# A four-layer graph network on one core: the weighted sum with turned probabilities stationary, and projections in two fp16 passes

## What is computed

```python
h = relu(layernorm(x)); x = x + L0(h)      # and so on for L1, L2, L3
# L0, one head: softmax over the neighbours of q.k / 8, times v
Q, K, V = h @ W_q, h @ W_k, h @ W_v
out = softmax(where(adj == 0, -1e9, Q @ K.T / 8)) @ V
# L1, four heads, with biases
q = h @ Wq[head] + bq[head]                # k and v the same way
scores = leaky_relu(q @ k.T / 8, 0.2) + mask
out = leaky_relu(mean_over_heads(softmax(scores) @ v), 0.2)
# L2, additive: e[i,j] = sum_f a[f] * leaky_relu(u[i,f] + w[j,f]);  out = elu(softmax(e) @ hp)
# L3: e[i,j] = leaky_relu(src[i] + dst[j]); out = norm(elu(softmax(e) @ Wh + h @ W_res)) * gamma + beta
```

## Time and profile before

| | us |
|---|---|
| median of 3 runs | 3885.69 (3883.1 to 3893.41) |
| profiled execution | 3882.72 |
| its span, first to last instruction | 3880.8 |
| PE, DVE, ACT, POOL busy | 3269.0, 3276.1, 3046.8, 992.1 |
| four-head layer's loop | 1026 |
| additive layer's loop | 2066 |
| last layer's loop | 367 |

### The profile page before, as it was taken

How to read it: one execution, slowest core, us unless ns; L and a number is a source line. 1 busy time by engine, 2 the same in 40 slices (tenths; PEclk the granted TensorE clock), 3 DMA queues, 4 the chain that set the end, 5 groups by cost and what they waited for, 6 DMA issues and landing times. The chain is left out here.

```text
span 3880.8 us, 81004 instructions
## 1 busy us (share of the span) xinstructions
PE 3269.0 (84%) x31339; PEld 1730.1 (45%) x31339; DVE 3276.1 (84%) x6456; ACT 3046.8 (79%) x3649; POOL 992.1 (26%) x565
## 2 busy tenths in 40 slices
PE   7997999999999968888788887887887878878776
PEld 5664666666666633233232232332322322226665
DVE  7776887888888778999999899899999998975776
ACT  3444777777777769899899998998999989975665
POOL 4333555555555600000000000000000000005664
PEclk9998999999999989999999999999999999998887
DMA  6550000000000000000000000000000000001111
GB/s 188 176 172 21 18 18 18 18 18 18 18 18 18 17 10 9 8 11 10 9 9 7 9 12 7 9 12 7 11 8 9 11 8 9 12 4 50 52 52 44
DMA packets 65885, 110.39 MB, mean 28 GB/s; under 512 B 24563, under 2 KB 24564, under 8 KB 65524
## 3 DMA queue, kind: packets, MB, share of 16 engines
q1 hardware_dynamic: 65524, 105.44, 9.0%
HBM read 86.55 MB, written 18.87 MB: 27 GB/s over the span
## 5 line engine op out<-in xcount | busy, mean ns | idle before, releaser
L919 ACT ACTIVATE l_scalar_ring<-l_w,l_r 128x1024 f32<-128x1024 f32 x1728 | 1812.9, 1143 | 33.1 <-DVE l_values L965 25.8
L1018 DVE TENSOR_SCALAR l_vector_ring<-l_w_code,l_r_code 128x1024 f32<-128x1024 f32 x2368 | 1621.6, 758 | 3.3 <-issue 0.4
L849 PE MATMUL scores<-l_scalar_ring,l_signs 128*32 128x512 f32 x6912 | 849.5, 610 | 91.5 <-ACT l_scalar_ring L919 91.4
L859 PE MATMUL scores<-l_vector_ring,l_signs_code 128*32 128x512 f16 x9472 | 657.1, 399 | 260.6 <-DVE l_vector_ring L1018 255.3
L226 ACT COPY probs_t<-turned 128x512 f32<-128x512 f32 x512 | 293.0, 586 | 508.3 <-PE turned L196 505.1
L407 POOL TENSOR_TENSOR l_masked<-l_relu,mask 128x1024 f32<-128x1024 f32 x256 | 545.7, 2132 | 489.1 <-ACT l_relu L531 456.2
L207 PE MATMUL outT<-probs_t,l_values 128*64 128x128 f32 x7168 | 514.5, 284 | 48.5 <-ACT probs_t L226 28.5
L859 PEld LDWEIGHTS scores<-l_vector_ring,l_signs_code 128*32 128x32 bf16 x9472 | 222.2, 96 | 735.5 <-DVE l_vector_ring L1018 496.3
L207 PEld LDWEIGHTS outT<-probs_t,l_values 128*64 128x64 f32 x7168 | 404.0, 140 | 283.4 <-DVE l_acc L615 110.3
L196 PE MATMUL turned<-ident,l_probs 128*128 128x128 f32 x3072 | 433.7, 286 | 11.1 <-issue 7.0
L849 PEld LDWEIGHTS scores<-l_scalar_ring,l_signs 128*32 128x32 f32 x6912 | 206.7, 111 | 493.4 <-issue 292.6
(11 more groups left out here) (207 smaller groups left out, 3284.8 us busy)
## 6 DMA issues: line engine op xcount, KB each, us to landing
mask<-masks_kept SPq DMA_DIRECT2D x192, 256.0 KB, 2.6
l_adj<-adj SPq DMA_DIRECT2D x64, 512.0 KB, 4.2
masks_kept<-mask SPq DMA_DIRECT2D x64, 256.0 KB, 2.3
x_res<-x SPq DMA_DIRECT2D x8, 256.0 KB, 5.0
out<-x_res SPq DMA_DIRECT2D x8, 256.0 KB, 3.4
l_wqk<-L_gnn_Wq SPq DMA_DIRECT2D x2, 64.0 KB
l_wqk<-L_gnn_Wk SPq DMA_DIRECT2D x2, 64.0 KB
l_wv<-L_gnn_Wv SPq DMA_DIRECT2D x1, 64.0 KB
```

The source lines that it names most:

```text
L849: last = nc.tensor.matmul(s.scores[g * ROWS:(g + 1) * ROWS, buf, half, :], signs[:, window], scalar_ring[:, at % SCALAR_RING, g, halves[ha ...
L859: last = nc.tensor.matmul(s.scores[g * ROWS:(g + 1) * ROWS, buf, half, :], signs_code[:, par, window], parts(vector_ring[:, at % VECTOR_RI ...
L919: last = nc.scalar.activation(scalar_ring[:, at % SCALAR_RING, g, :], w[:, par, :], ACT.Relu, bias=r[:, par, column:column + 1])
L1018: last = nc.vector.tensor_scalar(vector_ring[:, at % VECTOR_RING, g, :], w_code[:, par, :], r_code[:, par, column:column + 1], None, ALU.max)
```

## The change

The weighted sum. `probs_t` (128x128) is now stationary, and the values move. They have a 65th column of ones, so that the product is the output as it is needed, with the row's sum beside it. `turned_out`, `add_halves`, `copy_out`, `turn_out` and `rowsum` are gone, and `exponentials` no longer accumulates. `finish` waits for the product itself. In `dot_layer` it moves ahead of the half copy on DVE; in `additive_layer` it comes after set 15 of the next unit, where it was after set 1 of the one behind.

```diff
 def probs_times_values(pe, s, sems, values, u, out, buffers=1):
     pe.wait_ge(sems["half0_copied"], STARTS + u + 1)
     pe.wait_ge(sems["half1_copied"], STARTS + u + 1)
-    wait(pe, sems["out_copied"], STARTS + u)
+    wait(pe, sems["unit_done"], STARTS + u + 1 - buffers)
     for j in range(s.NB):
-        half = j % 2
-        last = s.nc.tensor.matmul(s.outT[half * s.D:(half + 1) * s.D, 0:P], values[:, j, :], s.probs_t[:, j, :],
-                                  start=(j < 2), stop=(j >= s.NB - 2))
+        last = s.nc.tensor.matmul(out[:, 0:s.D + 1], s.probs_t[:, j, :], values[:, j, :], start=(j == 0),
+                                  stop=(j == s.NB - 1), skip_group_check=True)
...
-def turn_out(pe, s, sems, u, fills_done, to=None, buffers=1):
...
-def copy_out(v, s, sems, u):
...
-    s.nc.scalar.activation(probs, logits, ACT.Exp, bias=s.negmax[:, slot:slot + 1], scale=scale,
-                           accum_out=s.rowsum[:, slot:slot + 1]).then_inc(sems["probs_ready"], 1)
+    s.nc.scalar.activation(probs, logits, ACT.Exp, bias=s.negmax[:, slot:slot + 1], scale=scale
+                           ).then_inc(sems["probs_ready"], 1)
```

```diff
@@ fill, on PE
-                    last = turn_y(pe, s, par, k, bank)
+                    for i in range(NB // 2):
+                        for twice in range(2):
+                            last = nc.tensor.matmul(bank[twice * D:(twice + 1) * D, i * P:(i + 1) * P],
+                                                    s.y[:, par, k * NB // 2 + i, :], up[:], start=True, stop=True,
...
-                    last = nc.tensor.matmul(bank[:, 0:WIDTH], wqk[:, p, :, :].rearrange("p a d -> p (a d)"),
-                                            s.hT[:, piece * WIDTH:(piece + 1) * WIDTH], start=True, stop=True)
+                    for part in (w_high, w_low):
+                        last = nc.tensor.matmul(bank[:, 0:WIDTH], part[:, which, h, :, :].rearrange("p a d -> p (a d)"), h2[:, cols],
+                                                start=(part is w_high), stop=(part is w_low))
@@ take_fill, on DVE
+                    last = nc.vector.scalar_tensor_tensor(out=low, in0=bank[rows, 0:WIDTH], scalar=qk_bias[rows, which, h:h + 1],
+                                                          in1=high, op0=ALU.add, op1=ALU.subtract)
...
-                    last = nc.vector.tensor_copy(values[:, par, at:at + each, :, :].rearrange("p j h d -> p (j h d)"), bank[:])
+                    for i in range(each if leaky else 1):
+                        if leaky:
+                            last = nc.vector.scalar_tensor_tensor(
@@ graph, on DVE
-                    copy_half(v, nc.vector.tensor_copy, s, sems, 0, u)
                     if n > 0:
                         finish(b, n - 1, u - 1)
+                    copy_half(v, nc.vector.tensor_copy, s, sems, 0, u)
```

More of the change, by code:

```diff
@@ L333, in fills_before, with weight_bank @@
             return min(K, n if leaky else n + n // 5)
+        def weight_bank(o):
+            return s.scores[:, 1, 1, 0:H * D] if o == 2 else s.out[:, o * H * D:(o + 1) * H * D]
         def steps_fills(n, project):
@@ L820, in _, with fill @@
         def _(pe):
[L821 removed]
+            def fill(b, par, k):
                 bank = fill_bank(s, b, k)
                 wait_for_bank(pe, s, sems, b, K, k, 0 if k < 2 else 4 if 4 <= k < 8 else 2)
[L824 removed]
                 both = [slice(h * BANK, (h + 1) * BANK) for h in range(2)]
@@ L1172, in gat_layer @@
         total = sb("total", [P, 8, NB], F32)
-        unit_out = [s.scores[:, 1, i, :] for i in range(2)]
+        unit_out = [s.scores[:, 1, i, 0:D + 1] for i in range(2)]
         block = ctx.enter_context(nc.Block())
@@ L1289, in fill, with graph @@
                 last.then_inc(sems["fill_ready"], 1)
-            def graph(b, par, project, first=False):
+            def graph(b, par, project):
                 for n in range(NB):
@@ L1306, in _ @@
                 fill(0, 0, k)
-            graph(0, 0, True, first=True)
+            graph(0, 0, True)
             with pe.Fori(0, (B - 4) // 2) as t:
```

276 lines of the change are left out of this document (147 added, 129 removed).

## The result

The changed kernel takes 3940.72 us (median, 3928.8 to 3942.19), the kernel before 3889.55 (3883.1 to 3897.38): a ratio of 1.0124, with a 95% interval from 1.0095 to 1.0153. It is slower, where the prediction said 3863 us and faster. The profiled execution took 3942.19 us, with a span of 3940.4.

What follows compares the result with a forecast made beforehand. PE was taken to bound the four-head layer, DVE nearly full, with DVE and ACT late by turns in the additive layer. Terms 41 - 100 - 2 + 23 + 16 = -22 gave 3863 us (chance 0.52), range 3812 to 3915.

Steps and rivals of the forecast that it cites:

- The weighted sum on PE, 1.82 us: Sum's sixteen records on PE take 1.82 us for 1.03: +0.79 in each of 448 units, -0.18 for the dropped turn.
- the fourth rival: Weight loads not hidden on PE: the sum takes 2.4 us for 1.82, +260, kernel 4120 us; chance 0.03.
- Units with a projection: Four-head layer, 22 of 32 units per graph: PE alone 4.04 us for 3.95, fp16 projection 0.43 for 0.95.
- the second rival: Four-head layer: sum, finish, copy, sum ring closes if logits start later than about 2.9 us after transposes; 3918 us, chance 0.17.
- Every fourth unit: Four-head units that also write x: 0.8 us more ahead of the half copy, 0.6 showing, taken as +0.12.
- +41: Four-head layer's total: +31 us for seven graphs and +10 for the last; bounds +15 to +90.
- Slower rival: Same as the second rival: finish ahead of half copy makes the next sum wait; 3918 us, chance 0.17.
- First layer, before the loops, last layer: Three smaller terms: first layer -2 us, work before the loops +16, longer sum on the last layer's chain +23.
- Additive layer, -100: DVE freed from the turn wait, sum wait and output copies: -100 us, between -60 and -150.
- +25: Additive layer: DVE enters its heavy half 3.6 us earlier per graph, seven graphs; beside 71 (DVE relief) and 6 (ACT).
- the ceiling: Rival: additive layer gains all of ACT's waits, -150 us, kernel 3813 us; chance 0.15.
- ACT pacing: Rival: ACT paces the whole additive layer, so only -60 us there, kernel 3903 us; chance 0.13.

Runs made afterwards that it cites:

- old_sum_fp16_projections: Changed kernel with the old weighted sum, output copy, turn and DVE order in the dot and last layers, fp16 projections kept: 3813.59 us, ratio 0.9806.
- x_from_psum: Changed kernel with l_leaked and x_res of the last head's finish reading one operand from PSUM, mean and scaling left out: 3868.06 us, ratio 0.9968.

## Why the prediction was wrong, point by point

**What bounds the kernel.** Right: PE without gaps in the four-head layer beside a nearly full DVE, late turns in the additive layer. That PE was not the only bound there showed when PE alone was relieved (old_sum_fp16_projections).

**The weighted sum on PE, 1.82 us.** Right: 1.81 to 1.84 from the first record to the next transposes where PE came to it after a wait, and 1.73 where it came without one. Loads that aren't hidden, the fourth rival, didn't happen.

**Units with a projection.** Right for the ordinary ones: 3.91, where PE alone had 4.04, and 4.24 in the unit ahead of every fourth. The logits start 1.7 to 2.8 us after the transposes' start in 98 of these 112 units (2.99 before; 2.7 was worked out, though 3.0 less 0.2 is 2.8), so the second rival's condition of 2.9 was met only in the 14 others, and in 35 of 42 every-fourth units, where they stand behind the held finish. Without a projection 3.66 for 3.61.

**Every fourth unit: this step failed.** I wrote "I take +0.1 for ordinary and +0.12 for these", from a finish with the block's part at 1.30 us. Those rows are of a finish behind the half copy, at the end of POOL's sum. The edit moved it ahead, under the first half of that sum, and I priced the two instructions at their old durations. For their length alone that price was right: where they are not held (x_from_psum) such a unit takes 4.61 us with a projection for 3.91, near the 0.6 that I gave. Held, it takes 5.24. Without a projection it is 5.24 for 3.95. Of the 98 us of the layer, 91 go when these two instructions move behind the copy: 70 with POOL's hold and the low clock behind it, the 21 others for plain length, the drains and `x_res` ahead of the copy. That last part is a remainder, not measured by itself. What is left in this layer with the finish split, +7 us, is less than the +41 I gave it: over seven graphs units 4 to 21 are 8 us shorter than before, where I had them longer, and those without a projection are even. Units 0 to 3, which hold the doubled transposes and the held `stat` scalings, cost 12 us, where I had about 3.

POOL's mask sum stood in the earlier trace rows, 402.57 and 2.14, and I read it only as what the logits wait for. In the kernel before, `l_leaked` was already stretched to as much as 0.61 us in 25 of 64 blocks, and no row of the prediction shows one.

**Slower rival.** It had the place right, "finish stands ahead of the half copy", and nearly the time (3918), but another mechanism: it asked when the logits start. What decided was the finish itself, at a quarter of the units. That its sum came near the measured time is luck.

**First layer, before the loops, last layer.** -3.7 for -2, +11.2 for +16, +23.2 for +23 and 2.8 at the tail. The last one is right by mechanism at the full clock (0.67 a unit for 0.8); the rest of it is the low clock, which I had named and not priced. The 5.6 us at the step to the additive layer scatter: kernels with the same code there have 84 to 90.

**Additive layer, -100.** Measured -78, and -83 alone. DVE's wait at the finish went from 91.2 us to nearly nothing, as predicted (1600 to 3450 us of the changed kernel):

```profile
ACT probs_t L213 <- PE turned L194: 66.0, 25, 3.7
...
DVE probs_t L213 <- PE turned L194: 27.8, 21, 3.2
...
ACT l_logits L236 <- DVE negmax L228: 10.8, 14, 1.2
...
DVE rinv L1101 <- PE unit_out L204: 8.5, 8, 1.1
```

Here the mechanism was right and the size was off: ACT still waits 77 us for 139, where I expected under 60, and DVE waits 27.8 us for the transposes, 1.4 before. DVE that runs ahead then stands for them. The term that was mis-sized is most likely the "+25" for entering the heavy half ahead: without it the sum is 71 + 6 = 77, for 78 measured. No run takes it by itself. The kernel with this layer alone agrees: there these two waits for the transposes are 63.9 and 27.8 us.

**Chances.** The forecast, the ceiling and ACT pacing took 0.80 together, and no case had a DVE instruction grow by what another engine does. The range ended at 3915, 26 us short.

## What to carry to other kernels

Before an instruction is moved, look at what runs on POOL at its new place: a DVE instruction with both operands in the on-chip memory, and in this case `stat`'s scaling with one, ended when POOL's did, so ahead of a copy that PE waits for it can cost up to the whole POOL instruction. Split such a finish: what frees the bank goes first, the rest behind the copy; and when a change's gain may come from a place in the order as much as from a new form, try the place alone, since one number gave three quarters of it here.

## What the runs showed of the hardware

- A DVE instruction (128x64, fp32) with two operands in the on-chip memory, started beside a POOL instruction that works there, ended 0.07 to 0.09 us after it in 55 of 55 cases, for a duration of up to 1.52 in place of 0.23 us; with one operand in PSUM it took 0.22 or 0.23 in 55 of 55.
- A DVE scaling of 128x8 fp32 numbers (TENSOR_SCALAR), one operand and the result in the on-chip memory, took 0.17 us alone and 0.60 to 2.15 us when it started beside a POOL instruction, in 10 of 10 cases of the changed kernel's four-head layer; each time it ended 0.03 us after POOL. A TENSOR_SCALAR of 128x1 took 0.21 or 0.22 us either way. One of 128x1024 took 1.5 to 1.8 us for 0.75 in 38 cases of the changed kernel's additive layer, all beside a POOL instruction.
- After PE had waited 1.5 us for the half copy, its granted clock was in some cases at the lower level for a part of the next unit: 21 units of the four-head layer had slow transposes, 17 of them right behind such a unit, for 3 before, and with the wait gone it was 3 again. In the last layer, with 1.2 us idle in units of 4.06, it stayed there for rows of units, 6.56 us each.
- Eight fp32 products with 128x128 stationary and 65 columns moving take 1.73 us to the next transposes at the full clock when PE comes to them without a wait, and 1.81 to 1.84 after one, where 128x64 stationary and 128 moving in two column halves took 1.02 or 1.03.
